# A fused attention and convolution kernel: blocks of local scores moved ahead of two projections, maxima moved ahead of the mask's steps

## The reference

```python
x = x + attention(group_norm(x))      # HiLo attention, 256 -> 256 channels
x = x + masked_conv(group_norm(x))    # 3x3 convolution, 256 -> 256 channels
```

## Time and profile before

| | |
|---|---|
| median of three runs | 343.78 us (343.34 to 344.1) |
| the profiled execution's own time | 342.3 us |
| its span, first to last instruction | 340.5 us |
| TensorE (PE) busy | 308.1 us, 91% |
| VectorE (DVE) busy | 270.1 us, 79% |
| ScalarE (ACT) busy | 148.8 us, 44% |
| GpSimd (POOL) busy | 87.4 us, 26% |
| mean granted clock of TensorE | 0.994 |

### The profile page before, as it was taken

How to read it: one execution, slowest core, us unless ns; L and a number is a source line. 1 busy time by engine, 2 the same in 40 slices (tenths; PEclk the granted TensorE clock), 3 DMA queues, 4 the chain that set the end, 5 groups by cost and what they waited for, 6 DMA issues and landing times.

```text
span 340.5 us, 4168 instructions
## 1 busy us (share of the span) xinstructions
PE 308.1 (91%) x1566; PEld 219.1 (64%) x1566; DVE 270.1 (79%) x489; ACT 148.8 (44%) x189; POOL 87.4 (26%) x47
## 2 busy tenths in 40 slices
PE   0998688999799899999799999997999999999995
PEld 1586252488666644887477727886688637878883
DVE  3989699689998687889987769789697667896562
ACT  2553488455726365450258734550354424121300
POOL 6089445214190200009600200029301100202000
PEclk9999999999999999999999999999899999999999
DMA  8746120051000000340103000430001001001003
GB/s 279 284 150 207 39 88 6 0 186 48 0 4 2 0 5 2 124 168 2 65 0 125 1 4 2 157 138 2 4 0 64 0 0 64 0 0 64 0 0 123
DMA packets 12547, 20.48 MB, mean 60 GB/s; under 512 B 2544, under 2 KB 8560, under 8 KB 12272
## 3 DMA queue, kind: packets, MB, share of 16 engines
q1 hardware_dynamic: 12528, 20.23, 16.5%
HBM read 7.93 MB, written 4.19 MB: 36 GB/s over the span
## 4 chain that ended last, share of the span: by engine, by line
PE 51%; DVE 22%; POOL 11%; ACT 8%; issue 6%; DMA 1%; DVEq 0%; POOLq 0%
PE slot L1144 25%; PE cps L1176 14%; PE slot L1220 7%; POOL probs L393 6%; DVE l_max L876 3%; ACT probs L588 3%; PE cps L1220 2%; DVE mask L812 2%; DVE v_lo L842 2%; POOL mask L393 2%; POOL cw_lo L350 1%; PE cps L1144 1%; DMA xy<-x 1%; ACT xn_hi L468 1%; ACT p_w L636 1%
## 5 line engine op out<-in xcount | busy, mean ns | idle before, releaser
L1176 PE MATMUL cps<-v_hi,cw_hi 128*128 128x512 f32 (+1 forms) x144 | 57.6, 400 | 3.7 <-DVE v_lo L842 2.9
L1176 PE MATMUL cps<-v_hi,cw_lo 128*128 128x512 f32 (+1 forms) x144 | 57.8, 401 | 0.0
L1176 PE MATMUL cps<-v_lo,cw_hi 128*128 128x512 f32 (+1 forms) x144 | 56.4, 392 | 0.0
L393 POOL TENSOR_TENSOR probs<-q_w,k_w 128x1024 f32<-128x1024 f32 x14 | 33.0, 2386 | 79.5 <-DVE rw L805 72.3
L588 ACT ACTIVATE probs<-slot 128x1024 f32<-128x1024 f32 x32 | 31.5, 1022 | 14.0 <-PE slot L1144 13.8
L876 DVE TENSOR_REDUCE l_max<-slot 128x4 f32<-128x1024 f32 x32 | 36.8, 1214 | 0.0
L1176 PEld LDWEIGHTS cps<-v_hi,cw_hi 128*128 128x128 f32 x144 | 27.4, 190 | 12.9 <-issue 5.3
L1176 PEld LDWEIGHTS cps<-v_hi,cw_lo 128*128 128x128 f32 x144 | 27.5, 191 | 7.3 <-issue 2.2
L1176 PEld LDWEIGHTS cps<-v_lo,cw_hi 128*128 128x128 f32 x144 | 27.4, 190 | 4.9
L376 POOL TENSOR_TENSOR mask<-rw 128x1024 f32<-128x1024 f32 x8 | 15.2, 1909 | 56.6 <-DVE rw L805 56.6
L1144 PE MATMUL slot<-xn_hi,w_hi 128*128 128x512 f32 (+1 forms) x68 | 27.3, 401 | 0.8 <-DVE xn_lo L734 0.8
(11 more groups left out here) (198 smaller groups left out, 632.7 us busy)
## 6 DMA issues: line engine op xcount, KB each, us to landing
xy<-x SPq DMA_DIRECT2D x8, 512.0 KB, 3.7
out<-xy SPq DMA_DIRECT2D x8, 512.0 KB, 2.6
qs<-probs SPq DMA_DIRECT2D x12, 256.0 KB, 2.5
qs<-probs SPq DMA_DIRECT2D x24, 128.0 KB, 2.1
raw_cw<-conv_w SPq DMA_DIRECT2D x2, 1152.0 KB, 6.2
ks<-probs SPq DMA_DIRECT2D x12, 128.0 KB, 2.1
probs<-h_qkv SPq DMA_DIRECT2D x2, 192.0 KB, 3.9
probs<-l_kv SPq DMA_DIRECT2D x2, 128.0 KB, 3.7
```

The lines of the kernel that those rows point to most:

```text
L393: nc.gpsimd.tensor_tensor(product(b, j).rearrange("p (n w) -> p n w", n=NW), q_w[:].rearrange("p (n w) -> p n w", n=NW), k_w[:, j * G:(j + ...
L1176: ins = nc.tensor.matmul(cps[:, pos % 2, y0 * WT:y1 * WT], (cw_hi, cw_hi, cw_lo)[part][:, k, pos, dy + 1, o * P:(o + 1) * P], (v_hi, v_lo, ...
```

## The change

For b = 2 and b = 3 the front is written anew; the front of b = 1 gets a function of its own (`second_front`) with its old order, and b = 0 too (`first_local`).

TensorE: the blocks of local scores begin right behind the window queries' projection and nine convolution matmuls. The keys' projection goes in pieces of three matmuls behind the blocks 0 to 3, the values' in pieces of four behind the blocks 5 to 7 (class `Projection`), both into slot 2. The blocks now use two slots in turn in place of three. The counts of convolution matmuls are `FRONT = (9, 4, 5, 18, 6, 22)`; their sum is 64, as before. The group's means go behind the turning of the maxima, into slot 1.

VectorE: behind the row sums come the older convolution's results (V_LEFT and V_RIGHT for b = 3, V_RIGHT for b = 2, which stood before the front), then all eight maxima and their parts, one more older result (V_SUM), and only then the column sums, the normalisation and the mask's steps. The first part of the window softmax is separated from its rest by a tile of the convolution.

GpSimd: the products of b = 2 and 3 no longer wait for the mask's steps; the mask's sums still do. ScalarE: the normalisation and both rectifications stand behind the copy of the window scores.

```diff
@@ -75,7 +75,7 @@
 REST = (4, 3, 5, 3, 4, 8)
 
 
-FRONT = (0, 11, 0, 0, 4, 3, 3, 3, 3, 3, 6, 10, 18)
+FRONT = (9, 4, 5, 18, 6, 22)
 POOL_WAIT = 8
@@ -233,7 +233,7 @@
 
         def means_at(b, i):
 
-            return (slot[1] if i == 0 else slot[2] if b else cps)[:, 0]
+            return (slot[1] if i == 0 or b else cps)[:, 0]
 
         block = ctx.enter_context(nc.Block())
@@ -355,7 +355,7 @@
 
         def block_slot(b, n):
 
-            return LA_SLOT[n] if b else LA_FIRST[n]
+            return LA_SLOT[n] if b == 1 else n % 2 if b else LA_FIRST[n]
 
         def score_slot(b, i):
@@ -426,8 +426,8 @@
                 if not first:
                     pool.wait_ge(proj_pe, b * 5 + 5)
                 pool.wait_ge(qkv_sb, b * 3 + 2)
-                wait_count(pool, mask_c, b * N_MASK)
                 if b == 1:
+                    pool.wait_ge(mask_c, N_MASK)
                     mask_sum(0, 2)
                     pool.wait_ge(v_dve, KT)
                     pool.wait_ge(lv_pe, 1)
@@ -518,7 +518,7 @@
 
             def window_copy(b, i, projected):
 
-                src = (flat[2], flat[0], flat[1] if b else flat_cps)[i]
+                src = flat[2] if b > 1 else (flat[2], flat[0], flat[1] if b else flat_cps)[i]
                 act.wait_ge(proj_pe, projected)
                 nc.scalar.copy((q_w, k_w, v_w)[i][:], src).then_inc(qkv_sb, 1)
@@ -598,9 +598,8 @@
                     nc.scalar.copy(sel[:].rearrange("p a b -> p (a b)"), raw_sel).then_inc(sel_act, 1)
                 late = b + 1 == RING
                 projections(b, first)
-                if not first:
-                    normalise_y(b - 1, b + 1)
                 if b == 1:
+                    normalise_y(0, 2)
                     for k in range(KT):
                         rectify(0, k)
                     conv_high(0, 0)
@@ -613,12 +612,12 @@
                     for done in stacked_late:
                         act.wait_ge(done, (b + 1) * STACK_LATE)
                     input_moments(b + 1, probs)
-                if b > 1:
-                    rectify(b - 1, 0)
                 act.wait_ge(ssum_pe, b + 1)
                 nc.scalar.copy(q_w[:], flat_cps if first else flat[0]).then_inc(ssum_sb, 1)
                 if b > 1:
-                    rectify(b - 1, 1)
+                    normalise_y(b - 1, b + 1)
+                    for k in range(KT):
+                        rectify(b - 1, k)
                 if b == 1:
                     conv_high(0, 1)
                 act.wait_ge(soft_c, b * N_SOFT + SOFT_READ)
...
+            def front(b, older):
+
+                query_lo(b)
+                key_lo(b)
+                dve.wait_ge(y_ready, b * KT)
+                row_sums(b - 1)
+                conv_result(older, (V_RIGHT,) if older == 0 else (V_LEFT, V_RIGHT))
+                maxima(b, range(NB))
                 maxima_parts(b)
-                if first:
-                    normalisation(1, 0)
-                older_result(V_DIFF)
-                if not first:
-                    for k in range(KT):
-                        masked_image(b - 1, k)
-                    conv_tiles(b - 1, 0, 0)
-                window_maxima(b)()
-                if first:
-                    turned_taps(weights)
-                if not first:
-                    conv_tiles(b - 1, 1, 0)
-                older_result(V_LEFT)
-                if not first:
-                    for k in range(KT):
-                        conv_low(b - 1, k, 0)
-                    for k in range(KT):
-                        conv_tiles(b - 1, k, 1)
-                older_result(V_RIGHT)
-                if not first:
-                    for k in range(KT):
-                        conv_low(b - 1, k, 1)
+                conv_result(older, (POS + V_SUM,))
+                column_sums(b - 1)
+                normalisation(b - 1, 1)
+                mask_parts(b - 1)
+                conv_result(older, (POS + V_DIFF,))
+                for k in range(KT):
+                    masked_image(b - 1, k)
+                conv_tiles(b - 1, 0, 0)
+                rest_of_softmax = window_maxima(b)
+                conv_tiles(b - 1, 1, 0)
+                rest_of_softmax()
+                conv_result(older, (POS + V_LEFT,))
+                for k in range(KT):
+                    conv_low(b - 1, k, 0)
+                for k in range(KT):
+                    conv_tiles(b - 1, k, 1)
+                conv_result(older, (POS + V_RIGHT,))
+                for k in range(KT):
+                    conv_low(b - 1, k, 1)
@@ -1059,8 +1053,6 @@
                 residual(b, 1, 2)
                 if not first:
                     pooling(b + 1)
-                if not first:
-                    conv_result(b - 1, (V_RIGHT,) if b == 1 else (V_LEFT, V_RIGHT))
                 if first:
                     second_front(b + 1)
                 else:
...
+            class Projection:
+
+
+                def __init__(self, to, c0):
+                    self.to, self.c0, self.at = to, c0, 0
+
+                def more(self, n):
+                    for m in range(self.at, self.at + n):
+                        k, part = divmod(m, 6)
+                        i, part = divmod(part, 3)
+                        cols = slice(self.c0, self.c0 + P)
+                        ins = mm(self.to[:, i], (w_hi, w_hi, w_lo)[part][:, k, cols],
+                                 (xn_hi, xn_lo, xn_hi)[part][:, k, halves(i)], m % 6 % 3 == 0 and k == 0,
+                                 part == 2 and k == KT - 1)
+                    self.at += n
+                    if self.at == 12:
+                        ins.then_inc(proj_pe, 1)
...
             def front(b, conv):
-                starting = b == 1
-                fill = FRONT_1 if starting else FRONT
-                if starting:
-                    conv = Convolution(0)
 
                 def tile_ready(k):
                     pe.wait_ge(xhi_ready, b * KT + k + 1)
                     pe.wait_ge(xlo_ready, b * KT + k + 1)
 
                 project(slot[0], WLQ, tile_ready)
-                if starting:
-                    pe.wait_ge(y_ready, KT - 1)
-                    keys_of_sums()
-                else:
-                    if b == 2:
-                        conv.more(POOL_WAIT)
-                    pe.wait_ge(pool_c, pooled_by(b + 1) * N_POOL)
-                    pe.wait_ge(y_ready, b * KT - 1)
-                    pooled_projections()
+                if b == 2:
+                    conv.more(POOL_WAIT)
+                pe.wait_ge(pool_c, pooled_by(b + 1) * N_POOL)
+                pe.wait_ge(y_ready, b * KT - 1)
+                pooled_projections()
                 pe.wait_ge(y_ready, b * KT)
-                if starting:
-                    group_means(0, 1)
                 project(slot[2], WQ)
+                conv.more(FRONT[0])
                 pe.wait_ge(lq_dve, b + 1)
-                project(slot[0], WK)
-                conv.more(fill[0])
-                if b > 1:
-                    pe.wait_ge(qkv_sb, b * 3 + 1)
-                    group_means(b - 1, 1)
-                pe.wait_ge(lk_act, (b + 1) * 2 - starting)
-                pe.wait_ge(lk_dve, b + 1)
-                project(slot[1], WV)
-                conv.more(fill[1])
+                keys, rest_of_values = Projection(slot[2], WK), Projection(slot[2], WV)
                 for n in range(NB):
                     if n == 0:
                         pe.wait_ge(stacked, (b + 1) * STACK + b * SHIFTS)
-                        pe.wait_ge(qkv_sb, b * 3 + 2)
                     elif n == 1:
-                        pe.wait_ge(qkv_sb, b * 3 + 3)
-                    elif n == 2:
-                        pe.wait_ge(gn_c[1], (b - 1) * N_GN + 1)
+                        pe.wait_ge(lk_act, (b + 1) * 2)
+                        pe.wait_ge(lk_dve, b + 1)
                     else:
-                        pe.wait_ge(la_max, b * NB + n - 2)
+                        pe.wait_ge(la_max, b * NB + n - 1)
                     stacked_quarter(b, n)
                     block_scores(b, n)
-                    if starting and n == 2:
-                        values_of_sums()
-                    elif starting and n == 5:
-                        weights_ready()
-                    elif starting and n == 6:
-                        pe.wait_ge(lk_act, 4)
-                    conv.more(fill[2 + n])
+                    if n == 0:
+                        pe.wait_ge(qkv_sb, b * 3 + 1)
+                    elif n == 5:
+                        pe.wait_ge(qkv_sb, b * 3 + 2)
+                    if n < 4:
+                        keys.more(3)
+                    elif n == 4:
+                        conv.more(FRONT[1])
+                    else:
+                        rest_of_values.more(4)
+                conv.more(FRONT[2])
+                pe.wait_ge(qkv_sb, b * 3 + 3)
                 maxima_turned(b)
-                conv.more(fill[10])
+                group_means(b - 1, 1)
```

(107 more changed lines are left out.)

1 line of the change is left out of this document (removed).

## The result

The changed kernel takes 367.25 us (median of six runs, 366.02 to 368.52) against 343.10 us for the kernel before (six runs beside them): a ratio of 1.0703 (95% interval 1.0667 to 1.0739), 24.15 us slower. The forecast was 367.7 us, within 356 to 374. The profiled execution took 368.52 us, with a span of 366.7. Of its 26.2 us over the profiled execution of before, 1.6 lie ahead of the changed fronts, where TensorE had a lower granted clock in this execution; so each front is measured here from the end of its own query projection.

The account below looks back on a forecast made before the run. TensorE was taken to bound the kernel, VectorE's chain hardly behind. Image 3's 10.55, image 4's 10.35 and the low clock's 3.0 made 23.9 us on the profiled 342.3; on the median 343.78, 367.7 us, range 356 to 374.

Parts of the forecast that it names:

- Where TensorE waits: Both fronts: TensorE idle some 7 to 9 us for VectorE's low part; busy total unchanged within the clock's price, share some 84%.
- Start of the blocks: Fronts, behind query projection and nine convolution matmuls: blocks start at 146.5 (image 3), 222.0 (image 4, after a new 1.2 us wait).
- T: Moment when TensorE has issued the values' projection's last matmul: forecast 156.6 in image 3, 232.1 in image 4.
- The held column sums: VectorE in both fronts: five column sums, held by GpSimd's products, end at T + 12.6 instead of T + 6.0 unblocked.
- From there to E: Both fronts: normalisation, mask's steps, mask sums, masked images, tiles and softmax follow the column sums, giving T + 30.9.
- E: Moment when the new convolution's first matmul can start: forecast 187.5 in image 3 (10.55 later), 263.0 in image 4 (10.35 later).
- The low clock behind the wait: TensorE behind its idle time before the new convolution: low clock adds 1.5 us in each front, 3.0 together.
- No blocking: Rival: small VectorE operations are not held beside the products; E = T + 23.3, 8.7 us slower, 352.5 us; chance 0.12.
- Faster: Rival: VectorE's chain in time, E by T + 15.5 (image 3), T + 17.3 (image 4); 337.6 us; chance 0.06 with nothing.
- worse: Rival: four long waits each cost 1.5 us of clock, products wait for VectorE; some 3 us per front, 374 us; chance 0.08.
- The three other waits: TensorE's waits for the third product, fourth product and V_DIFF result; the worse rival had each cost 1.5 us of clock.

Follow-up runs that it names:

- e1: Changed kernel with GpSimd's four products of images 3 and 4 replaced by operations that only write to the same places: 356.0 us, ratio to before 1.0375.
- f3: Kernel before with the filler alone, six convolution matmuls moved ahead of the turning of the maxima: 342.80 us, ratio 0.9999.

## Why the prediction was right, point by point

*Where TensorE waits.* Right in the wait: its releaser is the low part, and it is 7.55 and 6.93 us long (7 to 9 was forecast). Not right in the busy total, which was to stay the same but for the clock's price: it grew by 14 us (308.1 to 322.2) with the same number of matmuls, and so its share fell to 88% and not to 84%. Some 6 us of that lies in the two fronts (32.57 against 28.98 us, and 34.34 against 31.58), above all in the window scores: in image 3 they took 1.9 us in one go before (164.93 to 166.87), and now, as the products come one by one, three times 1.9 us. The rest is the lower clock, ahead of the fronts and behind them.

*Start of the blocks, T.* The new wait in image 4 is 1.16 us against 1.2. From the query projection to T: 12.4 and 13.8 us against 12.2 and 13.4.

*The held column sums.* Their end is T + 11.8 against T + 12.6. That they and not a rule of order make this term is shown by e1: with writes alone the mask's steps end 5.3 us sooner. GpSimd's products lengthened by 1.4 us beside the sums; the forecast put that into its rival, and it did not make the sums later: products and sums together take 11.6 us (158.70 to 170.28), a little under the 9.41 + 2.91 = 12.3 that were added up. One row was read loosely: the held TENSOR_TENSOR of the earlier trace rows has 128x1 elements, not two in each partition.

*From there to E.* T + 30.1 in both fronts against T + 30.9. The fronts are 10.0 and 9.9 us longer against 10.55 and 10.35.

*The low clock behind the wait.* This term was mis-sized. Twelve convolution matmuls take 4.95 us from 188.56 to 193.51, and 5.14 us from 275.97 to 281.11, where 12 x 0.227 = 2.7 are due: 2.2 and 2.4 us, not 1.5 each. In image 4 the first pooled scores are slow too (0.85 us from 281.11 to the next matmul, 0.46 in image 3), which makes 2.8. The 1.5 was taken from a wait of 2.36 us. With it the sum is 10.0 + 9.9 + 2.2 + 2.8 = 24.9 us; the medians differ by 24.15. The fronts were forecast 1.0 us too long and the clock 2.0 us too cheap, so that the forecast came within 0.5 us is in part luck.

*The rivals.* "No blocking" is refuted by the changed kernel's own rows (9.0 us for the sums), and e1, which comes near to it, gave 356.0 where that rival said 352.5. The rival let the mask's sums hold nothing either; in e1 the masked images still take 4.05 us beside them, as in the earlier trace rows, some 1 us more in each front. "Faster" failed at its point: TensorE's list ended 7 us ahead of E. Of "worse", the longer products and the dearer clock came true; the clock is 2.0 us of it in all, and the products, as said, nothing. The three other waits that it named stayed short (0.63, 0.85 and 0.90 us in image 3) and cost no clock.

## What to carry to other kernels

What an operation costs depends on what the other engine does at that time: before swapping two groups of VectorE work, write down which of them reads two SBUF tensors and which reads PSUM, and when GpSimd runs. Two halves of a reordering can each look guilty and be so only together: each of them undone alone gave back under 2 us of 24. When a wait is filled, look for the next one in the same stage first; the filler paid only together with the two orders that took the next wait away.

## What the runs showed of the hardware

GpSimd's operations that only write did not hold VectorE's operations with two SBUF inputs: 1.20 us for one and 1.48 us for the next three beside writes, 3.28 and 5.53 us beside products. They did hold a TENSOR_SCALAR with one input of 128x2 elements: 1.01 us in place of 0.17. GpSimd is held as well: its four products took 10.80 us beside the sums, 9.37 beside the maxima. After TensorE had been idle for about 7 us, all of the next eleven to twelve matmuls ran at 1.2 GHz (0.41 us apart, not 0.23), and the clock cost 2.2 and 2.8 us; after 2.36 us idle it had cost 1.5 us. After 1.53 us idle, in the kernel before, no lower clock was seen. The length of one wait does not decide it: in f3, with the filler alone, the copy of the window scores was waited for 2.06 us in each front, and the granted clock behind that was 1.00 in image 3 (171.06 to 173.00) and 0.53 in image 4 (245.36 to 247.20).
